# A decoder layer on one core: queries without padding, spread over the partitions by DMA, and the gate moved into the second expert layer

## The reference

```python
def xattn(inputs_q, inputs_kv, Wq, Wk, Wv, bq, bk, bv, Wo, bo):
    q = einsum('bsd,dhf->bshf', inputs_q, Wq) + bq
    k = einsum('bsd,dhf->bshf', inputs_kv, Wk) + bk
    v = einsum('bsd,dhf->bshf', inputs_kv, Wv) + bv
    attn = softmax(einsum('bqhf,bkhf->bhqk', q / sqrt(HEAD_DIM), k))
    return einsum('bqhf,hfd->bqd', einsum('bhqk,bkhf->bqhf', attn, v), Wo) + bo

def ffn(x, gate_W, gate_b, W1, b1, g1, be1, W2, b2, g2, be2):
    topk_scores, topk_idx = top_k(xf @ gate_W + gate_b, 2)
    weights = softmax(topk_scores)
    def expert(w1, bb1, gg1, bbe1, w2, bb2, gg2, bbe2):
        h = relu(layernorm(xf @ w1 + bb1, gg1, bbe1))
        return layernorm(h @ w2 + bb2, gg2, bbe2)
    out = sum(weights[..., None] * all_out[topk_idx])
    return out + xf

x = layernorm(x + mamba(x, ...))
x = layernorm(x + xattn(x, ctx, ...))
x = layernorm(x + ffn(x, ...))
```

## Time and profile before

| | us |
|---|---|
| median of 3 runs | 1556.57 |
| lowest and highest | 1555.38, 1560.92 |
| the profiled execution, its own time | 1557.38 |
| the profiled execution, first to last instruction (span) | 1555.6 |

### The profile page before, as it was taken

One profiled execution on the slowest core, in us unless ns is written; L12 is line 12 of the kernel. 1 busy time (PEld: TensorE's weight loads), 2 busy tenths in 40 slices (PEclk: granted clock), 3 DMA queues, 4 the chain that ended last, 5 costly groups with the idle time before them and its releaser, 6 DMA issues. The chain is left out here.

```text
span 1555.6 us, 22512 instructions
## 1 busy us (share of the span) xinstructions
PE 1329.6 (85%) x7506; PEld 936.1 (60%) x7506; DVE 1365.8 (88%) x2507; ACT 1107.5 (71%) x2539; POOL 1007.1 (65%) x702
## 2 busy tenths in 40 slices
PE   7788788878877887887787888999999999999997
PEld 5667667766766676666665553547454735473465
DVE  6999999999999999999998762668978897888798
ACT  5977988898889889888987524246844684368475
POOL 3999999999999999999999711100750075007402
PEclk9899989899999999999998987999999999999999
DMA  6202211220222022112203004100001000000000
GB/s 222 76 2 75 89 30 61 90 89 4 86 89 76 15 89 89 33 57 89 83 3 108 15 14 170 59 1 1 1 28 59 1 1 28 28 1 1 1 28 28
DMA packets 46646, 78.52 MB, mean 50 GB/s; under 512 B 3841, under 2 KB 40290, under 8 KB 42306
## 3 DMA queue, kind: packets, MB, share of 16 engines
q1 hardware_dynamic: 46530, 77.08, 14.9%
HBM read 68.16 MB, written 8.91 MB: 50 GB/s over the span
## 5 line engine op out<-in xcount | busy, mean ns | idle before, releaser
L974 POOL TENSOR_TENSOR state_c<-state,c_area 128x1024 f32<-128x1024 f32 x256 | 600.8, 2363 | 17.1 <-DVE state L1053 13.4
L1053 DVE TENSOR_TENSOR_SCAN state<-decay,ps 128x512 f32<-128x512 f32 x384 | 463.4, 1210 | 3.2 <-ACT decay L725 1.5
L725 ACT ACTIVATE decay<-step_area,negA 128x255 f32<-128x255 f32 x768 | 324.6, 497 | 0.0
L1807 POOL TENSOR_TENSOR big<-big,g_sb 128x1024 f32<-128x1024 f32 x27 | 74.7, 2768 | 375.1 <-ACT big L1663 353.9
L425 PE MATMUL ps<-ident_sb,state_c 128*128 128x128 f32 x2048 | 287.4, 292 | 0.8 <-POOL state_c L974 0.8
L425 PEld LDWEIGHTS ps<-ident_sb,state_c 128*128 128x128 f32 x2048 | 257.0, 152 | 19.5 <-issue 8.2
L1021 DVE TENSOR_TENSOR ps<-step_area,ps 128x512 f32<-128x512 f32 x384 | 261.3, 680 | 6.6 <-PE ps L409 4.9
L941 POOL TENSOR_TENSOR ub<-step_area,b_bc 128x1024 f32<-128x1024 f32 x64 | 151.7, 2371 | 26.2 <-DMA b_bc<-bc_scratch 26.2
L1053 DVE TENSOR_TENSOR_SCAN state<-ps,ub 128x512 f32<-128x512 f32 x128 | 154.7, 1209 | 15.9 <-ACT ps L738 9.7
L409 PE MATMUL ps<-parts,sel_bc_sb 96*128 96x256 bf16 x192 | 55.6, 290 | 100.7 <-DVE ps L1037 89.2
L1548 PE MATMUL ps<-w_sb,weights 128*128 128x512 f32 x256 | 124.5, 622 | 0.8 <-ACT weights L1625 0.7
(11 more groups left out here) (237 smaller groups left out, 2474.3 us busy)
## 6 DMA issues: line engine op xcount, KB each, us to landing
c_area<-bc_scratch SPq DMA_DIRECT2D x32, 1024.0 KB, 10.0
b_bc<-bc_scratch SPq DMA_DIRECT2D x16, 512.0 KB, 6.3
weights<-in_xT SPq DMA_DIRECT2D x16, 256.0 KB, 3.0
res<-in_x SPq DMA_DIRECT2D x16, 256.0 KB, 2.8
x_scratch<-res SPq DMA_DIRECT2D x16, 256.0 KB, 5.7
weights<-x_scratch SPq DMA_DIRECT2D x4, 1024.0 KB, 8.8
xa<-x_scratch SPq DMA_DIRECT2D x4, 1024.0 KB, 5.5
out_x<-acc SPq DMA_DIRECT2D x3, 1024.0 KB, 4.5
```

The lines of the kernel that those rows point to most:

```text
L725: nc.scalar.activation(decay_tile(i, n)[:, j, 1:], dt_sb[:, i[1] % 2, j, 1:], ACT.Exp, scale=negA[:, j * NS + n:j * NS + n + 1]).then_inc( ...
L974: nc.gpsimd.tensor_tensor(state_c[:, n % RING, :, :], state[:, n % RING, :, :], c_bc[:, q, n, :].unsqueeze(1).to_broadcast([P, CT, TC]), A ...
L1053: nc.vector.tensor_tensor_scan(state[:, n % RING, pair, :].rearrange("p j n -> p (j n)"), a, b, 0.0, ALU.mult, ALU.add).then_inc(s_scan, 1)
```

## The change

In the turns with `more` (for batches 2 to 4):

- **Queries of 256 real columns.** A second weight `wqp`, without padding, is loaded at the start (256 KB). A batch's queries take 4 products instead of 8. ScalarE copies them to `q_flat`, a part of the tile `hT`. A bias without padding lies between the two old ones in `bqk`, which grows from 8 to 10 columns.
- **Spread by DMA.** SP waits for the copies of a half and then issues 8 DMAs from `q_flat` to `qT`, each for the 16 rows of a head in both groups of that half: 16 partitions times 2 rows of 2 KB, 64 KB. Ahead of them, 4 DMAs from a tensor of zeros clear the maximum's rows (one partition, 16 KB each). That is 20 DMAs a turn. SP issues the load of `xa` only after all of them.
- **Rounds.** TensorE runs all queries in a row, then the transposes of this batch's rows, then 2 rounds of maxima, and after these one piece a half tile, from the first half tile on. Round 0 waits for the first half's DMAs, round 8 for the second half's. The four DVE operations of the early rounds become two, behind `finished`; `final` is cut into three pieces (3, 3 and 2 tiles) behind the rounds of the first three half tiles.
- **Gate.** `gate` runs after the first four `turn_tiles` of the second expert layer, and `gate_scores` directly before `gate_ranks`.

The gate (L1538) has come between the transposes and the first product. The core of the diff:

```diff
+            def clear_maxima():
+                for j in range(HG):
+                    row = BLK * j + HD
+                    sp.dma_start(qT[row:row + 1, :, :].rearrange("p g n -> p (g n)"), zeros[j:j + 1, :]).then_inc(s_spread[0], 16)
+
+            def spread(b, half):
+                sp.wait_ge(s_qc, q_count(b, QG * (half + 1)))
+                tokens = slice(half * HALF, (half + 1) * HALF)
+                for a in range(G // QG):
+                    for j in range(HG):
+                        first = HD * (HG * a + j)
+                        sp.dma_start(qT[BLK * j:BLK * j + HD, a:G:G // QG, tokens],
+                                     q_flat[first:first + HD, QG * half:QG * (half + 1), :]).then_inc(s_spread[half], 16)
...
                     load_ctx(b + 1)
+                    sp.wait_ge(s_xt, (b + 1) * TRB + TRB)
+                    clear_maxima()
+                    for half in range(NL):
+                        spread(b + 1, half)
                     sp.wait_ge(s_r, b * TT + TT)
                     load_x1(b + 1, xa[:, :, :], s_x)
...
             def query(b, half, g):
-                v = half * G + g
-                if v == 0:
+                if half + g == 0:
                     pe.wait_ge(s_xtc, b * TRB + TRB)
-                elif v >= G:
-                    pe.wait_ge(s_qc, b * U + v - G + 1)
                 for k in range(KT):
-                    last = nc.tensor.matmul(ps[:, 4 + g, :], wq_sb[:, k, g * P:(g + 1) * P],
+                    last = nc.tensor.matmul(ps[:, 4 + QG * half + g, :], wqp_sb[:, k, g * P:(g + 1) * P],
                                             x1T[:, k, half * HALF:(half + 1) * HALF], start=k == 0, stop=k == KT - 1)
...
                 if r == 0:
-                    pe.wait_ge(s_kvc, b * KVB + KVB)
-                if r > free:
-                    pe.wait_ge(s_max, b * RB + r - free)
+                    pe.wait_ge(s_qc, q_count(b, NL * QG))
+                    pe.wait_ge(s_spread[0], b * 16 * (SPREADS + HG))
+                else:
+                    pe.wait_ge(s_max, b * RB + r)
                 if r == HB:
                     pe.wait_ge(s_qm, 2 * b * NL + 2)
+                    pe.wait_ge(s_spread[1], b * 16 * SPREADS)
...
-                    for g in range(G):
-                        query(b + 1, 0, g)
-                    for g in range(G):
-                        one_round(b + 1, work.pop(0), base=0)
-                        query(b + 1, 1, g)
-                    pe.wait_ge(s_max, (b + 1) * RB + EARLY)
+                    for half in range(NL):
+                        for g in range(QG):
+                            query(b + 1, half, g)
+                    pe.wait_ge(s_kvc, (b + 1) * KVB + KVB)
...
                     transposes(xt, 0, s_yt)
+                    for r in range(EARLY):
+                        one_round(b + 1, work.pop(0))
                     pe.wait_ge(s_ytc, b * TRB + TRB)
-                    pe.wait_ge(s_qc, (b + 1) * U + U)
-                    gate()
...
                     for c in range(2 * KT):
                         turn_tiles(c)
+                    if more and n == 0:
+                        gate()
```

More of the change, by code:

```diff
@@ L1150, in _, with attn_ffn_block @@
             round_neg(1)
-def attn_ffn_block(nc, x1, ctxT, ident_sb, w, w1, w2, ps, late, shared, bo, g2, be2, bias_rows, before, out):
+def attn_ffn_block(nc, x1, ctxT, ident_sb, w, w1, w2, ps, late, shared, bo, g2, be2, bias_rows, before, zeros, out):
     U = G * NL
@@ L1551, in turn @@
                             last.then_inc(s_l1, 1)
-                        if more and t == 0 and h == 0:
-                            pe.wait_ge(s_gd, b * GDB + 1)
-                        if work and 2 * t + h >= SKIP:
+                        if work:
                             one_round(b + 1, work.pop(0))
@@ L1562, in turn @@
                     pe.wait_ge(s_n1, b * TT + TG * (n + 1))
+                    if more and n:
+                        pe.wait_ge(s_gd, b * GDB + 1)
                     def turn_tiles(c):
@@ L1704, in turn @@
                     guess(b, 0)
-                    for u in range(U):
+                    for u in range(NL * QG):
                         query(b + 1, u)
@@ L1954, in final_stats, with final @@
                 nc.vector.bn_stats(fstats[:, t, :], acc[:, t, :]).then_inc(s_fst, 1)
-            def final(b):
-                for t in range(TT):
+            def final(b, tiles=range(TT)):
+                for t in tiles:
                     nc.vector.tensor_scalar(acc[:, t, :], acc[:, t, :], fmean[:, t:t + 1], frstd[:, t:t + 1],
@@ L2085, in turn @@
                 work = rounds() if more else []
-                for r in range(EARLY if more else 0):
-                    one_round(b + 1, work.pop(0), base=0)
+                ending = list(range(TT)) if more and tail else []
                 def finished():
@@ L2095, in turn @@
                     finished()
-                if more:
-                    gate_scores(b)
+                for r in range(EARLY if more else 0):
+                    one_round(b + 1, work.pop(0))
                 if more and tail:
                     final_newton(b - 1)
-                    final(b - 1)
                 def advance(slot):
-                    if work and slot >= SKIP:
+                    if work:
                         one_round(b + 1, work.pop(0))
+                    if ending:
+                        final(b - 1, [ending.pop(0) for _ in range(min(3, len(ending)))])
                 for t in range(TT):
@@ L2137, in turn @@
                 if more:
+                    gate_scores(b)
                     gate_ranks(b)
@@ L2248, in decoder_block @@
                     shared, w, ctxT)
-        attn_ffn_block(nc, x1, ctxT, ident_sb, w, channels(w1), channels(w2), ps, late, shared, bo, g2, be2, bias_rows, before, out)
+        attn_ffn_block(nc, x1, ctxT, ident_sb, w, channels(w1), channels(w2), ps, late, shared, bo, g2, be2, bias_rows, before, zeros, out)
 def _constants():
```

48 lines of the change are left out of this document (26 added, 22 removed).

## The result

| | before | after |
|---|---|---|
| median of 17 runs each, us | 1556.82 | 1561.42 |
| lowest and highest | 1554.52, 1560.92 | 1557.66, 1565.91 |
| profiled execution, time and span | 1557.38, 1555.6 | 1565.91, 1564.1 |

The ratio is 1.0028, with a 95% interval of 1.0018 to 1.0039: slower by 4.4 us, and within the 0.5% that the prediction called no change. The forecast was 1546.4 in a range of 1539 to 1556, so it was wrong: by 15 us, and on the other side of the kernel before.

The account below looks back on a forecast made before the run. TensorE was taken to bound the kernel. Gains less waits, gate and clock gave 3.66 us in the first turn and 3.26 in each other, 10.2 in all, from 1557.38 to 1547.2; less 0.8 for the median, 1546.4, range 1539 to 1556.

Parts of the forecast that it names:

- Part 1: First query to the third half tile's round: 26.87 us become 19.21 + W, a gain of 7.66 - W a turn.
- W: PE's wait ahead of round 0 for the spread DMAs: 0.8 us a turn, bounds 0.1 to 4.6.
- Part 2: DVE in the first half tiles: `final` fits between maxima except in the third step; PE waits 0.4 us in two turns.
- the third rival: First half tiles: POOL's addition holds DVE's `final`, some 3 us in two turns, 1552.4 us; chance 0.06.
- Part 3: Second expert layer: at the new place gate costs 1.0 us and `gate_scores` 0.7 a turn.
- Part 4: PE around the first rounds: idle time lowers the clock to 1.2 GHz for a while, costing 1.5 us a turn.
- The clock does not hold: Denies the rival that the clock stays up around the first rounds despite PE's waits: 1541.9 us, chance 0.22.
- The late landing: Rival ahead of round 0: spread DMAs land late, W = 3.3, 2.5 us more a turn, 1553.9 us; chance 0.10.
- SP's queue does not jam: Denies the rival that spread DMAs jam SP's queue at 1.5 us an issue, W = 7.8, 1567.5 us; chance 0.12.

Follow-up runs that it names:

- e5: Changed kernel with the load of `xa` issued ahead of the spread and gate and `gate_scores` back before the first expert layer; 1544.83 us, 0.9931 of before.
- e7: Changed kernel with `xa` loaded early and each query spread alone, 32 DMAs of 32 KB instead of 16 of 64; 1558.01 us, 1.0008 of before.
- e8: Changed kernel with each spread DMA cut to 128 of 512 tokens, SP alone issuing; only waits ahead of round 0 read: 2.10, 1.99, 2.00 us.
- e2: Changed kernel with gate and `gate_scores` back ahead of the first expert layer; 1555.67 us, 0.9999 of before.
- e3: Changed kernel with four of the first eight spread DMAs issued by ACT, beside SP; 1560.56 us, 1.0020 of before.
- e4: Changed kernel with three extra matmuls on constants filling PE's wait ahead of round 0, result overwritten; 1557.37 us, 1.0004 of before.
- e11: Changed kernel with spread DMAs cut to 128 of 512 tokens, ACT issuing four of the first eight; only waits read: none ahead of round 0.
- e9: Changed kernel with POOL's addition in 8 pieces instead of one, SP's order as changed; 1557.72 us, 1.0008 of before.
- e10: Kernel before with only gate and `gate_scores` moved to their new place in the second expert layer; 1564.94 us, 1.0059 of before.
- e1: Changed kernel with SP's load of `xa` issued ahead of the clears and spreads; 1554.55 us, 0.9987 of before.

## Why the prediction was wrong, step by step

The forecast was a sum over three turns, so it can be laid beside the traces term by term. From the first query to the round of the third half tile after has 23.51, 27.48 and 26.96 us; the prediction's base is 19.21, and the waits are read from the rows, so the remainder is the clock's. Part 1 is thus taken over as forecast; what bears it out stands below the table.

| term, us in three turns | forecast | measured |
|---|---|---|
| Part 1 without W, 7.66 a turn | -23.0 | -23.0 (taken over) |
| W | 2.4 | 2.66 + 2.52 + 2.49 = 7.7 |
| the clock, behind the first rounds | 4.5 | 1.6 + 2.3 + 3.1 = 7.1 |
| DVE late in the first half tiles | 0.8 | 3.44 + 2.15 = 5.6 |
| a second clock fall behind that wait | 0 | 1.66 + 1.64 = 3.3 |
| gate and `gate_scores` | 5.1 | 2.4 + 1.6 + 0.7 = 4.7 |
| sum | -10.2 | +5.3 |

**Part 1 was right.** Four queries in 7.14 us, the transposes at once, the second round 2.36 us after the first where the clock holds, and steps of 2.65. Where the clock holds for the whole stretch, in e5, it is 10.33 us from round 0 to the round of the third half tile, against a forecast of 2.35 + 7.97. In the first turn 19.21 + 2.66 leaves 1.6 for the clock, the forecast's 1.5.

**W failed, by 1.8 us a turn.** Half of it is the issue. I took 0.50 us from L262, and these DMAs cost 0.64, in e7 with half the bytes and in e8 with a quarter: the eighth starts 4.5 us after the copy and not 3.55. The other half is landing: 2.3 to 2.5 us, where I took 1.7 as nearest to the 32 KB store. The bounds of 0.1 to 4.6 held it. The choice near the lower end rested on size alone, though no row showed an SBUF to SBUF transfer of 16 partitions. The prediction's own mark, wrong if this wait is over 2 us, was met in every turn.

**Part 2 failed, and this is the largest step.** The step that failed is that `final` fits between the maxima: the forecast let it run at 0.33 us each. It was held by POOL's addition, as in the third rival: 3.44 us in one turn, 2.15 in the other. The rival's price of 3 us a turn was about right for the wait and left out the second clock fall, 1.65 each. Such a fall doesn't follow every time: of the 12 waits for DVE at this place in after, e2, e3, e4, e8 and e11 (2.00 to 3.70 us), 7 had one behind them and 5 had none, 3.60 and 3.59 among them. That the wait would come was to be read from the trace of before. I had shown L1831 only, which has two tensor inputs, and wrote that no row tells whether an operation with one is held. One does, 6 us later in the same timeline, DVE and then POOL of the kernel before:

```profile
1264.08 2.23 DVE L1848 TENSOR_SCALAR newt<-newt 128x16 f32<-128x16 f32 x1
```

```profile
1263.88 2.40 POOL L1807 TENSOR_TENSOR big<-big,g_sb 128x1024 f32<-128x1024 f32 x1
```

It is a TENSOR_SCALAR with a single tensor in SBUF, it needs 0.17 us elsewhere, and here it takes 2.23 and ends with POOL's instruction. In the same traces BATCH_NORM_STATS2 and STREAM_TRANSPOSE, and TENSOR_REDUCE and TENSOR_TENSOR with an input in PSUM, run beside POOL at their usual lengths. It is the kind of operation that decides, and `final` is of the kind of L1848.

The Trainium skill ("SBUF — State Buffer", "Who interferes with whom") names `tensor_scalar` among the operations that can run in a mode of two ports and are then shut out for the whole of a GpSimd instruction. Every run here agrees: held for 4.3 us by one instruction of 4.50, and for one piece at a time in e9. My reading of the rule failed, not the rule. I had set the 405 ns of `final` against the 284 of L2010 and taken the longer for one port, by which the third rival fell away.

**Part 3 was right in size.** 1.7 us a turn were forecast; 1.6, 1.6 and 2.1 are e10's, and e2 gives 2.4 and 1.6. But it was not asked what the old place costs. It costs nothing, in the kernel before because ACT's preset is late there (e10), and in the changed one because the spread is (e2). So this part of the change takes some 5 us by the table, and gives nothing.

**Part 4 was right in kind.** The fall comes in every turn in which W is 2 us or more (after, e1, e3, e8, e9), and in e7 behind 4.25 us ahead of round 1. With shorter waits it comes in some: with 0.80 and 1.56 us in three of four turns (e2, e5), with 1.36 and 1.56 in neither of two (e5), with the 1.55 alone in one of three (e11) and in none of three (e4). Its size is 1.5 to 3.1, against the forecast's 1.5.

**The other rivals.** The clock does not hold. The late landing (W = 3.3) was nearer to the truth than the forecast, but by itself it gives 1553.9. SP's queue does not jam: 0.64 us is not 1.5. (That the queue was full at the issue of 4.53 us in the earlier trace rows was my reading; the trace shows only that it stood behind an issue of 5.05 us and the 1 MB load of the tokens that this one started.) The slower side was forecast by one mechanism and came by another: W, the clock and the wait for DVE, each of which had a range or a rival of its own, all went to the dear end, my range took them one at a time, and the second clock fall had no term at all.

**What stays open.** In the third turn the part behind the first is 1.3 to 1.5 us shorter than before wherever the gate is at its old place in the changed kernel (184.7 and 184.9 against 186.2 us in e2 and e5). But e8, with the gate at its new place, has 184.8 there too, where after has 186.9, so the gate's place does not explain it, and no run tells why. e10's median is 2.5 us above what its trace shows behind the scan stage. And the DVE wait is 3.4 us in the second turn and 2.2 in the third, which I put down to SP's and PE's times shifting against each other; that is not shown. The traces of e2, e4 and e8 have 3.51, 3.60 and 3.59 in the second turn and 3.27, 2.75 and 3.70 in the third, so after's sum of 5.6 is the lowest of the four.

## What to carry to other kernels

Before an operation is moved beside another engine's, look in the trace for the same kind of operation at a place where both run, and compare its longest with its shortest time; a mean hides it. A transfer that is put between two engines costs its issues first, so count them at the price of the nearest kind, and ask in what order the queue serves what stands behind them. And before a piece of work is moved away because it takes time, see what the engine would wait for in its place: the gate was free where it stood.

## What the runs showed of the hardware

- An issue of an SBUF to SBUF DMA of 16 partitions costs SP 0.64 us from one to the next, whether it moves 16, 32 or 64 KB. The four clearing DMAs of one partition each cost 1.14 us together.
- From issue to landing, such a DMA takes 2.3 us with 64 KB, 2.0 with 32 and 1.8 with 16. Issued from two queues at once, 64 KB ones took up to 4.4 us until PE went on, and 16 KB ones made no wait.
- Single issues can take longer: up to 900 ns on SP and 862 on ACT while both queues issued, but also 947 in e7, where SP alone did, so these lengths don't show that the queues hinder each other's issues. The Trainium skill ("Perfetto Trace Analysis", "DMA Instruction — HWDGE (DVE, Sync)") counts a wait for exclusive use of the descriptor generator into this time. No run here shows such a wait apart from other causes.
- The clock falls to 1.2 GHz even amid dense work (0.56 granted in 7.3 us of after). 2.0 to 2.7 us of waiting, a round of 0.81 and 1.55 us more brought it down in every turn; 0.80, the same round and 1.56 did so in three turns of four, 1.36 and 1.56 in neither of two. The length of the waits alone doesn't tell whether it falls: a single wait of 3.60 us passed without a fall (e4), one of 2.13 had one in one turn of e10 and none in another.
